# A graph network's second edge pass: rows prescaled by the attention vector, sums and absolute values on ScalarE

## The chip, the cores and the metric

The kernel runs on one core of a Trainium2 chip (trn2). The time is that of one execution on the device, in microseconds (us); the median of several runs counts.

## What is computed

Two graph layers over the same 103125 edges (50000 random ones in both directions and 3125 loops), 3125 nodes and 256 features; the edges come sorted by their destination.

```python
x = _layernorm(x + layer0(x, src, dst))      # attention with 8 heads over edges, then an MLP with GELU
x = _layernorm(x + layer1(x, src, dst))

def layer1(feature, src, dst, W_s, W_t, W_attn, W_fc, b_fc):
    proj_s = feature @ W_s.T
    proj_t = feature @ W_t.T
    z = proj_s[src] + proj_t[dst]
    z = where(z >= 0, z, 0.2 * z)
    e = (z @ W_attn.T)[:, 0]                 # one number an edge
    e_exp = exp(e - segment_max(e, src)[src])
    alpha = e_exp / segment_sum(e_exp, src)[src]
    msg = feature[src] * alpha[:, None]
    return segment_sum(msg, dst) @ W_fc.T + b_fc
```

The change lies in `e`, the edge score of layer 1, and in the tables of rows that it reads.

## The kernel before

One program, its engines coupled by semaphores that are written out by hand; nothing is scheduled by a tool. The stages, with their place in the profiled execution:

- 0 to 150 us: tables of the graph, and the q, k, v rows of layer 0, stored as rows in DRAM.
- 150 to 1535: **pass one**, the edges of layer 0.
- 1535 to 1890: **node stage**, five batches of 5 x 128 nodes: MLP, norms, and the two projections of layer 1. Per 128 nodes ScalarE copies both from PSUM (L1305, L1306) into `row` and `target`, VectorE multiplies both by 0.2 x attn and sums them (L1640, L1642) into one column more each; `split` (L1464 and the line behind) cuts `target` into three bfloat16 parts, and SyncE stores `row` and `x1` as `proj_rows` (514 float32 an edge's source), `row` alone as `narrow_rows` (258), and the parts as `part_rows`.
- 1890 to 3136: **pass two**, the edge scores of layer 1.
- 3136 to 3826: **pass three**, weighted sums of features by destination, output.

An edge tile is 128 edges, one per partition. A **visit** is 30 tiles, taken as 15 pairs p = 0 to 14; pass two has 27 visits. In a visit of pass two:

- GpSimd issues one indirect gather per tile (`gather_pair`, L793), 18 of wide rows of `proj_rows` and 12 of `narrow_rows`, into 15 pair slots (rooms `sb_ring`, `sb_w`, `sb_slots`). The gather for pair p of a visit may start when pair p of the visit before has been used (`slots_free`). It is thus up to a visit ahead.
- ScalarE makes the one-hot matrices that pick the destination node of each edge (`node_distances` L1178, `node_onehots` L1183; five of each, 768 columns), a visit ahead, and one Exp (L1324) for the visit before.
- TensorE expands the destination's part rows to edges with those one-hots (`expand`, L916): six matmuls a pair, three parts each, into PSUM `px`. It runs up to three pairs ahead of VectorE. At the last five pairs it also adds 6 matmuls each of the softmax denominators of the visit before (`denominators`, L1052).
- VectorE, per pair: `rows(p)` (L1699) adds gathered row and expanded row into `zbuf` (five pairs deep) and frees slot and PSUM; `attend(p)` copies the two extra columns (COPY, L1704) and makes one product with accumulator per tile (L1706): max(z, 0) x 0.8 attn. The leaky relu is 0.2 z + 0.8 max(z, 0), and the first term comes summed from the node stage in that extra column. Another extra column says if the edge's destination lies in the visit's window of nodes. Between the pairs stand `weighed` steps for the visit before, by the table `WEIGHED`: `low` (L1683, a comparison over 3840 columns), `high` (L1668), the split of the exponentials in three parts and `spread` (L1687, 2250 columns). Behind pair 14 come four operations on 30 columns (L1730, L1732, L1733, L1738).
- SyncE loads indices, destinations and part rows, and writes the source's features from `proj_kept` to `x_edges` for pass three.

Each engine works through its own queue in order; the order of the work around the change is the order in which these functions are written.

## Time and profile before

| | |
|---|---|
| runs | 3196.54, 3208.22, 3199.06 us |
| median | 3199.06 us |
| span of the profiled execution | 3825.7 us (19.6% over the median) |
| busy in it: TensorE, VectorE, ScalarE, GpSimd | 2265.8, 2190.3, 1162.1, 2033.0 us |
| DMA | 698.67 MB in 365776 packets |

The profiled execution has no time of its own beside its span. The span is read from the records of the engines; the runs were timed without a profile. In the rows below PE is TensorE (matmul), PEld its weight load, DVE VectorE, ACT ScalarE, POOL GpSimd, SP SyncE, and a "q" behind a name is the engine's sequencer. The bracket behind a row of a timeline, or what stands behind the second bar of a group, is the idle time ahead and what ended it. L793 is line 793 of the kernel before.

### The profile page before, as it was taken

The page shows a single profiled execution, that of the slowest core. Times are in us where ns is not written, and L with a number is a line of the kernel's source. Part 1 is how long each engine was busy: PE and PEld are TensorE (multiplying, and loading weights), DVE is VectorE, ACT ScalarE, POOL GpSimd, SP SyncE. Part 2 cuts the span into 40 slices and gives each one's busy share as a digit, 9 for nine tenths or more (in the row PEclk, how much of TensorE's full clock was granted, in tenths as well). Part 3 has the DMA queues.
Part 4 walks back from the last instruction along what each step waited for, and adds up shares of the span by engine and source line. Part 5 has one row for each costly group of instructions (what it writes and reads, how often), then busy time and mean ns, then how long its engine had stood idle before and what let it go on. Part 6 is the DMA issues. An engine that isn't in the chain of part 4 may idle for free.

```text
span 3825.7 us, 55082 instructions
## 1 busy us (share of the span) xinstructions
PE 2265.8 (59%) x11461; PEld 1680.5 (44%) x11462; DVE 2190.3 (57%) x6388; ACT 1162.1 (30%) x2751; POOL 2033.0 (53%) x1970
## 2 busy tenths in 40 slices
PE   4566666666666666587534445444444446777777
PEld 2244444444454444475423323332322235565565
DVE  5466556565665666234245556555555576666766
ACT  0145545554554555243212212222222210111111
POOL 0255555555565554212366676767776635444443
PEclk9788878887888788798766666666666668889988
DMA  4666666666666664122477777777777765666665
GB/s 139 208 174 183 177 184 185 179 185 181 185 183 188 187 181 129 54 69 74 139 205 217 219 218 216 213 212 216 212 213 215 211 209 187 194 193 199 202 199 171
DMA packets 365776, 698.67 MB, mean 183 GB/s; under 512 B 77382, under 2 KB 247104, under 8 KB 365739
## 3 DMA queue, kind: packets, MB, share of 16 engines
q0 software_dynamic: 134784, 425.63, 38.2%
q1 hardware_dynamic: 220666, 256.40, 21.4%
q10 hardware_dynamic: 10288, 16.23, 1.2%
q8 instruction: 12, 0.20, 0.0%
q14 instruction: 26, 0.21, 0.0%
HBM read 597.23 MB, written 100.85 MB: 182 GB/s over the span
## 4 chain that ended last, share of the span: by engine, by line
PE 31%; another core or an unknown queue 23%; DVE 21%; issue 16%; DMA 3%; DVEq 2%; SPq 2%; ACT 1%; POOL 1%; ACTq 0%; POOLq 0%
PE ps_px L916 10%; DVE sb_score L1517 4%; PE ps_pa L929 3%; PE ps_px L929 3%; DVE sb_prod L1706 3%; PE ps_pn L1052 3%; PE ps_px L1014 2%; DVE sb_wide L1699 2%; PE ps_px L1023 2%; PE ps_pa L1093 2%; DVE sb_wide L1526 1%; PE ps_px L892 1%; DVE sb_prod L1511 1%; DVE sb_parts L1911 1%
## 5 line engine op out<-in xcount | busy, mean ns | idle before, releaser
L916 PE MATMUL ps_px<-sb_parts 128*128 x2430 | 457.1, 349 | 609.8 <-DVE sb_wide L1699 465.4
L916 PEld LDWEIGHTS ps_px<-sb_parts 128*128 128x128 bf16 x2430 | 276.8, 121 | 757.2 <-DVE sb_wide L1699 490.7
L793 POOL DMA_INDIRECT sb_ring<-proj_rows,sb_idx x324 | 360.5, 1113 | 281.8 <-issue 164.1
L793 POOL DMA_INDIRECT sb_ring<-kv_rows,sb_idx x324 | 320.4, 989 | 338.4 <-DVE sb_wide L1526 131.5
L929 PE MATMUL ps_pa<-sb_wide,sb_onehot 128*128 128x264 f32 x864 | 300.5, 480 | 260.4 <-DVE sb_wide L1526 201.3
L793 POOL DMA_INDIRECT sb_parts<-kv_rows,sb_idx x324 | 316.0, 975 | 204.0 <-DVE sb_wide L1526 102.1
L916 PE MATMUL ps_px<-sb_parts,sb_xwm 128*128 x2430 | 399.9, 310 | 31.6 <-issue 14.8
L793 POOL DMA_INDIRECT sb_w<-narrow_rows,sb_idx x324 | 348.7, 1076 | 101.0 <-issue 97.5
L929 PE MATMUL ps_px<-sb_wide,sb_onehot 128*128 128x264 f32 x756 | 257.9, 474 | 201.6 <-DVE sb_wide L1526 141.0
L1699 DVE TENSOR_TENSOR sb_wide<-ps_px,sb_ring 128x516 f32<-128x516 f32 x162 | 109.6, 687 | 431.1 <-remote 392.2
L916 PEld LDWEIGHTS ps_px<-sb_parts,sb_xwm 128*128 128x128 bf16 x2430 | 271.4, 112 | 163.9 <-issue 63.3
L929 PEld LDWEIGHTS ps_pa<-sb_wide,sb_onehot 128*128 128x128 f32 x864 | 183.6, 234 | 315.7 <-DVE sb_wide L1526 189.1
L1197 ACT ACTIVATE sb_onehot<-sb_bits 128x256 f32<-128x256 bf16 x405 | 165.6, 409 | 489.8 <-remote 326.1
L793 POOL DMA_INDIRECT sb_w<-feat_rows,sb_idx x162 | 158.2, 977 | 293.5 <-PE ps_px L1093 132.0
L1706 DVE SCALAR_TENSOR_TENSOR sb_prod<-sb_wide,sb_attn_hi 128x256 f32<-128x256 f32 x810 | 309.1, 417 | 0.0
L1178 ACT ACTIVATE sb_parts<-sb_bits,sb_nn_tab 128x768 bf16<-128x768 int16 x135 | 126.0, 935 | 578.1 <-PE ps_px L916 397.7
L1190 ACT ACTIVATE sb_bits<-sb_iota_w,sb_ndst_f 128x128 bf16<-128x128 f32 x810 | 278.1, 389 | 39.7 <-issue 26.2
L1517 DVE TENSOR_REDUCE sb_score<-sb_prod 128x16 f32<-128x512 f32 x405 | 272.9, 674 | 0.0
L929 PEld LDWEIGHTS ps_px<-sb_wide,sb_onehot 128*128 128x128 f32 x756 | 160.4, 234 | 250.2 <-issue 117.4
L1911 DVE TENSOR_SCALAR sb_parts<-sb_iota_n,sb_dst_g,sb_ex_g 128x128 f32<-128x128 f32 x810 | 219.0, 355 | 35.6 <-issue 34.3
L1511 DVE TENSOR_TENSOR sb_prod<-ps_px,sb_ring 128x512 f32<-128x512 f32 x162 | 111.0, 685 | 221.0 <-remote 118.7
L1511 DVE TENSOR_TENSOR sb_prod<-ps_px,sb_parts 128x512 f32<-128x512 f32 x162 | 110.8, 684 | 208.5 <-remote 145.4
(265 smaller groups left out, 4535.1 us busy)
## 6 DMA issues: line engine op xcount, KB each, us to landing
sb_bits<-dst_short SPq DMA_DIRECT2D x280, 192.0 KB
x_edges<-sb_ring SPq DMA_DIRECT2D x54, 768.0 KB
sb_slots<-x_edges SPq DMA_DIRECT2D x54, 768.0 KB
x_edges<-sb_slots SPq DMA_DIRECT2D x27, 768.0 KB
sb_w<-x_edges SPq DMA_DIRECT2D x27, 768.0 KB
sb_msg<-lo_rows SPq DMA_DIRECT2D x28, 576.0 KB
kv_rows<-sb_slots ACTq DMA_DIRECT2D x25, 256.0 KB, 2.9
sb_parts<-part_rows SPq DMA_DIRECT2D x28, 193.5 KB
```

Source lines behind the costliest of these rows:

```text
L793: pool.indirect_dma_start(out=out[:, i, :], out_offset=None, in_=rows, in_offset=bass.IndirectOffsetOnAxis(ap=idx[:, 2 * p + i:2 * p + i + ...
L916: mm = pe.matmul(into, hots_t[L][:, 2 * p + i, :], flat(visit_parts[:, bass.ds(parity, 1), a, 0:width]), start=(a == 0), stop=(a == 2))
L929: mm = pe.matmul(into[:, 0:C + H], onehot[:, j, :], sums_in[:, 2 * (p % FLIGHT) + i, :], start=(p % EARLY == 0 and i == 0), stop=True, ski ...
L1052: mm = pe.matmul(pn[:, 0:3 * W], lo_hot[:, :, j], hi_ex[:, :, :, j].rearrange("p a n -> p (a n)"), start=False, stop=True, skip_group_chec ...
L1178: act.activation(hots_t[L][:, half(h), :], drow[:, h], ACT.Abs, bias=nn_tab[:, bass.ds(v, 1)]).then_inc(far[L], 1)
L1190: ins = act.activation(away[:, j, :], iota_w[:], ACT.Abs, bias=ndst_f[:, bass.ds(t0 + (2 * p + i), 1)])
L1197: act.activation(onehot[:, places(p), :], away[:, places(p), :], ACT.Relu, bias=1.0, scale=-1.0).then_inc(hot[0], 1)
L1511: dve.tensor_tensor(prod[:, p % 3].rearrange("p (j c) -> p j c", j=2), px[:, p % FLIGHT, :].rearrange("p (j c) -> p j c", j=2), kv_pairs[p ...
L1517: dve.tensor_reduce(score[:, p % FLIGHT], prod[:, p % 3].rearrange("p (j h d) -> p j h d", j=2, h=H), AX, ALU.add).then_inc(red1, 1)
L1699: dve.tensor_tensor(zbuf[:, pair(p), :], px[:, places(p), 0:CW], proj_slots(p)[:, :, 0:CW], ALU.add).then_inc(slots_free[1], 1)
L1706: ins = dve.scalar_tensor_tensor(out=prod[:, p % 3, i * C:i * C + C], in0=zbuf[:, 2 * (p % FLIGHT) + i, 0:C], scalar=0.0, in1=attn_hi[:], ...
L1911: ins = dve.tensor_scalar(weights[:, j, :], iota_n[:], dst_g[:, j:j + 1], ex_g[:, j:j + 1], ALU.is_equal, ALU.mult)
```

## The change

- In the node stage VectorE multiplies both projections by attn on their way out of PSUM; ScalarE's copies and the two products with accumulator are gone, and so are the two extra columns. Rows are 512 and 256 wide.
- Since z is now already z x attn, the leaky score is 0.6 x sum(z) + sum(|z| x 0.4 sign(attn)). ScalarE makes the first sum (Identity with accumulator into `lines`, two of 256 columns a pair; its other output goes to `unread`) and |z| (Abs, 512 columns, into `msg`); VectorE's two products now take |z| and `attn_sign`. New semaphores `lined` (ScalarE to VectorE) and `attended` (back).
- Whether the destination lies in the visit's window is now worked out on VectorE from the destination's number (`dst`, `above`, `inside`).
- PSUM holds five pairs ahead, one bank each, instead of three.
- The denominators are three matmuls a pair from p = 3 to 12, for the visit two back.
- The `weighed` steps move from p = 1 to 7 to p = 7 to 12. ScalarE's one-hots stand between its pairs.
- GpSimd gets a wait on the expansion (`expanded`) at p = 0, 5 and 10.

```diff
-CW = C + 2
-ROW = CW + C
+ROW = 2 * C
+EVEN = (1.0 + SLOPE) / 2.0
+ODD = (1.0 - SLOPE) / 2.0
...
-        attn_lo = sb("attn_lo", [P, C])
-        attn_hi = sb("attn_hi", [P, C])
+        attn_sign = sb("attn_sign", [P, C])
...
+        unread = onehot[:].rearrange("p j e -> p (j e)").bitcast(BF16).rearrange("p (j c) -> p j c", j=R)
         dots = sb("dots", [P, 3, G])
-        low_dots = sb("low_dots", [P, 2, G])
+        lines = sb("lines", [P, G])
...
-        NAS, NA = batch_steps(["hT*", "hid*", "sqrt1", "x1T*", "rows*"])
+        NAS, NA = batch_steps(["hT*", "hid*", "sqrt1", "x1T*"])
-        ZS = steps(["dots", "low", "masked", "kept", "added"])
+        ZS = steps(["dst", "above", "inside", "both", "masked", "kept", "added"])
...
+            def expanded(L, v, p):
+
+                pool.wait_ge(expd[L], v * PAIRS + p + PAIRS)
+                pool.sem_inc(pool_seen, 1)
...
                             pool.wait_ge(idx_in[1][p // SLOTS], v * 16 + 16)
+                            expanded(1, v, p)
...
-                    pe.wait_ge(slots_free[1], v * PAIRS + p + 1 + PAIRS - RING)
+                    pe.wait_ge(slots_free[1], v * PAIRS + p + 1 + PAIRS - FLIGHT)
-                    into = px[:, p % FLIGHT, i * C:i * C + width] if L == 0 else px[:, 2 * (p % RING) + i, 0:width]
+                    into = px[:, p % FLIGHT, i * C:(i + 1) * C]
...
-                for j in range(g * R, (g + 1) * R):
+                for j in range(g * THIRDS, (g + 1) * THIRDS):
...
-            def scored(v, earlier=None, second=False):
+            def scored(v, before=None, second=False):
-                    expand(1, CW, parity, v, p)
-                    if second and p == 2:
+                    expand(1, parity, v, p)
+                    if second and p == 7:
                         top_transposed()
-                    if second and p == 4:
+                    if second and p == 9:
                         top_spread()
-                    if earlier is not None and p >= PAIRS - HALVES:
-                        denominators(earlier, p - (PAIRS - HALVES))
+                    if before is not None and 3 <= p < 3 + S:
+                        denominators(before, p - 3)
...
-                scored(pe.snap(u + 2), pe.snap(u + 1))
-            for g in range(HALVES):
-                denominators(last_visit(pe), g)
+                scored(pe.snap(u + 2), u)
+            for v in (visit_before(pe), last_visit(pe)):
+                for g in range(S):
+                    denominators(v, g)
...
-                for s in range(NB):
-                    after_pe(it, "proj", s)
-
-                    act.wait_ge(proj_stored, it * (32 * NB) + 1)
-                    act.copy(row[:, s, 0:C], px[:, s % 4, 0:C])
-                    act.copy(target[:, s, 0:C], px[:, s % 4, C:2 * C]).then_inc(na, 1)
...
-            def node_half(v):
-                for h in range(HALVES):
-                    node_distances(1, v, h)
-                    if h:
-                        node_onehots(1, v, h - 1)
-                node_onehots(1, v, HALVES - 1)
+            def lined_up(v, p):
+
+                act.wait_ge(slots_free[1], v * PAIRS + p + 1 + PAIRS)
+                act.sem_inc(act_seen, 1)
+                act.wait_ge(attended, v * PAIRS + p + 1)
+                for i in (0, 1):
+                    act.activation(unread[:, 2 * (p % RING) + i], zbuf[:, 2 * (p % FLIGHT) + i, :], ACT.Identity, accum_out=lines[:, 2 * p + i:2 * p + i + 1])
+                act.activation(msg[:, places(p), 0:C], zbuf[:, pair(p), :], ACT.Abs).then_inc(lined, 1)
...
-            node_half(0)
-            with act.Fori(0, total - 1) as u:
-                node_half(act.snap(u + 1))
-                score_exps(u)
+            def scored(v, after=None, earlier=None):
+                for p in range(PAIRS):
+                    if p == 0 and earlier is not None:
+                        act.wait_ge(zs, earlier * len(ZS) + ZS["both"])
+                        act.sem_inc(act_seen, 1)
+                    lined_up(v, p)
+                    if earlier is not None and p == 6:
+                        score_exps(earlier)
+                    if after is not None and p % RING == 1 and p > 1:
+                        node_distances(1, after, p // RING - 1)
+                    if after is not None and p % RING == 2 and p > 2:
+                        node_onehots(1, after, p // RING - 1)
+                if after is not None:
+                    node_distances(1, after, HALVES - 1)
+                    node_onehots(1, after, HALVES - 1)
+
+            for h in range(HALVES):
+                node_distances(1, 0, h)
+                node_onehots(1, 0, h)
+            scored(0, 1)
+            with act.Fori(0, total - 2) as u:
+                scored(act.snap(u + 1), act.snap(u + 2), u)
+            scored(last_visit(act), earlier=visit_before(act))
...
-            dve.tensor_scalar(attn_lo[:], attn[:], SLOPE, None, ALU.mult).then_inc(tables, 1)
-            dve.tensor_scalar(attn_hi[:], attn[:], 1.0 - SLOPE, None, ALU.mult).then_inc(tables, 1)
+            dve.tensor_scalar(attn_sign[:], attn[:], 0.0, 2.0 * ODD, ALU.is_gt, ALU.mult).then_inc(tables, 1)
...
+            dve.tensor_scalar(attn_sign[:], attn_sign[:], -ODD, None, ALU.add).then_inc(tables, 1)
...
-                    dve.wait_ge(na, it * NA + NAS["rows", s])
-                    dve.scalar_tensor_tensor(out=prod[:, 0, 0:C], in0=px[:, s % 4, 0:C], scalar=1.0, in1=attn_lo[:], op0=ALU.mult, op1=ALU.mult,
-                                             accum_out=row[:, s, C:C + 1])
-                    dve.scalar_tensor_tensor(out=prod[:, 1, 0:C], in0=px[:, s % 4, C:2 * C], scalar=1.0, in1=attn_lo[:], op0=ALU.mult, op1=ALU.mult,
-                                             accum_out=target[:, s, C:C + 1]).then_inc(ndot, 1)
-                    dve.wait_ge(ndot, it * NB + s + 2)
-
-                split(target, CW, (W // NB + it) * SPLITS + 1, W // NB + it)
+                    dve.wait_ge(nt, it * NT + NTS["proj", s])
+                    dve.tensor_tensor(row[:, s], px[:, s % 4, 0:C], attn[:], ALU.mult)
+                    dve.tensor_tensor(target[:, s], px[:, s % 4, C:2 * C], attn[:], ALU.mult).then_inc(ndot, 1)
+
+                dve.wait_ge(ndot, it * NB + NB + 1)
+                split(target, C, (W // NB + it) * SPLITS + 1, W // NB + it)
...
-                    dve.wait_ge(dpe, v * HALVES + HALVES)
+                    dve.wait_ge(dpe, v + 1)
...
-            WEIGHED = {1: ["low"], 3: ["ex"], 4: ["part0"], 5: ["left1"], 6: ["part1", "high"], 7: ["left2", "part2", "spread"]}
+            WEIGHED = {7: ["ex"], 8: ["part0"], 9: ["left1", "low"], 10: ["part1", "high"], 11: ["left2"], 12: ["part2", "spread"]}
...
-                    dve.tensor_tensor(zbuf[:, pair(p), :], px[:, places(p), 0:CW], proj_slots(p)[:, :, 0:CW], ALU.add).then_inc(slots_free[1], 1)
+                    dve.tensor_tensor(zbuf[:, pair(p), :], px[:, p % FLIGHT, :].rearrange("p (j c) -> p j c", j=2),
+                                      proj_slots(p)[:, :, 0:C], ALU.add).then_inc(slots_free[1], 1)
                 def attend(p):
-                    dve.wait_ge(slots_free[1], v * PAIRS + p + 1 + PAIRS)
-                    dve.tensor_copy(low_dots[:, :, 2 * p:2 * p + 2].rearrange("p c j -> p j c"), zbuf[:, pair(p), C:CW])
+                    dve.wait_ge(lined, v * PAIRS + p + 1)
                     for i in (0, 1):
-                        ins = dve.scalar_tensor_tensor(out=prod[:, p % 3, i * C:i * C + C], in0=zbuf[:, 2 * (p % FLIGHT) + i, 0:C], scalar=0.0, in1=attn_hi[:],
-                                                       op0=ALU.max, op1=ALU.mult, accum_out=dots[:, 0, 2 * p + i:2 * p + i + 1])
-                    if p == PAIRS - 1:
-                        ins.then_inc(zs, 1)
+                        ins = dve.scalar_tensor_tensor(out=prod[:, p % 3, i * C:i * C + C], in0=msg[:, 2 * (p % RING) + i, 0:C], scalar=1.0, in1=attn_sign[:],
+                                                       op0=ALU.mult, op1=ALU.mult, accum_out=dots[:, 0, 2 * p + i:2 * p + i + 1])
+                    ins.then_inc(attended, 1)
...
                 rows(0)
+                rows(1)
                 for p in range(PAIRS):
-                    if p + 1 < PAIRS:
-                        rows(p + 1)
+                    if p + 2 < PAIRS:
+                        rows(p + 2)
                     attend(p)
-                    if second and p == 0:
+                    if p < 3:
+                        inside(("dst", "above", "inside")[p])
...
-                dve.wait_ge(zs, at("dots"))
-                dve.tensor_tensor(dots[:, 1], dots[:, 0], low_dots[:, 0], ALU.add).then_inc(zs, 1)
-                dve.wait_ge(zs, at("low"))
-                dve.tensor_tensor(dots[:, 2], dots[:, 1], low_dots[:, 1], ALU.mult).then_inc(zs, 1)
-                dve.tensor_copy(kept, low_dots[:, 1]).then_inc(zs, 1)
+                dve.wait_ge(attended, v * PAIRS + PAIRS + RING)
+                dve.scalar_tensor_tensor(out=dots[:, 0], in0=lines[:], scalar=EVEN, in1=dots[:, 0], op0=ALU.mult, op1=ALU.add).then_inc(zs, 1)
+                dve.wait_ge(zs, at("both"))
+                dve.tensor_tensor(dots[:, 2], dots[:, 0], dots[:, 1], ALU.mult).then_inc(zs, 1)
+                dve.tensor_copy(kept, dots[:, 1]).then_inc(zs, 1)
                 dve.wait_ge(zs, at("kept"))
```

Three places show how the instructions stand. **ScalarE**, in the loop of pass two. Before, at the start of a visit's turn: the distances (L1178) and one-hots (L1183) of the next visit follow each other.

```order
L1176 ISA [waits drow_in1_0]
L1178 ISA [waits expd1]
L1178 ACT_TABLE_LOAD
L1178 ACTIVATE sb_parts<-sb_bits,sb_nn_tab 128x768
L1176 REGISTER_ALU [waits drow_in1_1]
L1178 ACTIVATE sb_parts<-sb_bits,sb_nn_tab 128x768 [waits expd1]
L1182 ISA
L1183 ACTIVATE sb_parts<-sb_parts 128x768 [waits far1]
L1176 REGISTER_ALU [waits drow_in1_2]
L1178 ACTIVATE sb_parts<-sb_bits,sb_nn_tab 128x768 [waits expd1]
L1182 REGISTER_ALU
L1183 ACTIVATE sb_parts<-sb_parts 128x768 [waits far1]
```

After (L1324 is the sum, L1325 the absolute value, L1188 the distances, L1193 the one-hots):

```order
L1325 ACTIVATE sb_msg<-sb_wide 128x2x256
L1185 ISA
L1186 ISA [waits drow_in1_0]
L1188 ISA [waits expd1]
L1188 ACTIVATE sb_parts<-sb_bits,sb_nn_tab 128x768
L1320 REGISTER_ALU
L1322 REGISTER_ALU [waits slots_free1]
L1324 ACTIVATE sb_onehot,sb_lines<-sb_wide 128x256 [waits attended]
L1324 ACTIVATE sb_onehot,sb_lines<-sb_wide 128x256
L1325 ACTIVATE sb_msg<-sb_wide 128x2x256
L1192 ISA
L1193 ACTIVATE sb_parts<-sb_parts 128x768 [waits far1]
```

Each group of distances and one-hots now stands behind the sums of a pair and ahead of the next one's.

**VectorE**, pairs in the middle of a visit. Before (L1699 row add, L1704 copy of the extra columns, L1706 product):

```order
L1699 TENSOR_TENSOR sb_wide<-ps_px,sb_w 128x2x258 [waits gathered10,expd1]
L1704 COPY sb_low_dots<-sb_wide 128x2x2 [waits slots_free1]
L1706 SCALAR_TENSOR_TENSOR sb_prod,sb_dots<-sb_wide,sb_attn_hi 128x256 x2
L1699 TENSOR_TENSOR sb_wide<-ps_px,sb_w 128x2x258 [waits gathered11,expd1]
L1704 COPY sb_low_dots<-sb_wide 128x2x2 [waits slots_free1]
L1706 SCALAR_TENSOR_TENSOR sb_prod,sb_dots<-sb_wide,sb_attn_hi 128x256 x2
L1699 TENSOR_TENSOR sb_wide<-ps_px,sb_slots 128x2x258 [waits gathered12,expd1]
L1704 COPY sb_low_dots<-sb_wide 128x2x2 [waits slots_free1]
L1706 SCALAR_TENSOR_TENSOR sb_prod,sb_dots<-sb_wide,sb_attn_hi 128x256 x2
```

After (L1723 row add, L1730 product):

```order
L1723 TENSOR_TENSOR sb_wide<-ps_px,sb_w 128x2x256 [waits gathered9,expd1]
L1730 SCALAR_TENSOR_TENSOR sb_prod,sb_dots<-sb_msg,sb_attn_sign 128x256 [waits lined]
L1730 SCALAR_TENSOR_TENSOR sb_prod,sb_dots<-sb_msg,sb_attn_sign 128x256
L1723 TENSOR_TENSOR sb_wide<-ps_px,sb_w 128x2x256 [waits gathered10,expd1]
L1730 SCALAR_TENSOR_TENSOR sb_prod,sb_dots<-sb_msg,sb_attn_sign 128x256 [waits lined]
L1730 SCALAR_TENSOR_TENSOR sb_prod,sb_dots<-sb_msg,sb_attn_sign 128x256
L1723 TENSOR_TENSOR sb_wide<-ps_px,sb_w 128x2x256 [waits gathered11,expd1]
L1730 SCALAR_TENSOR_TENSOR sb_prod,sb_dots<-sb_msg,sb_attn_sign 128x256 [waits lined]
L1730 SCALAR_TENSOR_TENSOR sb_prod,sb_dots<-sb_msg,sb_attn_sign 128x256
```

The copy is gone, and the product waits for ScalarE in place of VectorE's own row add.

**TensorE**, denominators. Before, at the last pairs of a visit:

```order
L916 MATMUL ps_px<-sb_parts 128x258 [waits slots_free1]
L916 MATMUL ps_px<-sb_parts 128x258 x5
L1052 MATMUL ps_pn<-sb_parts 128x75 x6
L912 REGISTER_ALU
L916 MATMUL ps_px<-sb_parts 128x258 [waits slots_free1]
L916 MATMUL ps_px<-sb_parts 128x258 x5
L1052 MATMUL ps_pn<-sb_parts 128x75 x6
```

After, at p = 3 to 5 (L924 expansion, L1060 denominators):

```order
L924 MATMUL ps_px<-sb_parts 128x256 [waits slots_free1]
L924 MATMUL ps_px<-sb_parts 128x256 x5
L1058 REGISTER_ALU
L1060 MATMUL ps_pn<-sb_parts 128x75 [waits dv]
L1060 MATMUL ps_pn<-sb_parts 128x75 x2
L920 REGISTER_ALU
L924 MATMUL ps_px<-sb_parts 128x256 [waits slots_free1]
L924 MATMUL ps_px<-sb_parts 128x256 x5
L1060 MATMUL ps_pn<-sb_parts 128x75 x3
L920 REGISTER_ALU
L924 MATMUL ps_px<-sb_parts 128x256 [waits slots_free1]
L924 MATMUL ps_px<-sb_parts 128x256 x5
L1060 MATMUL ps_pn<-sb_parts 128x75 x3
```

Six behind each of five pairs became three behind each of ten, and the wait for VectorE's weights (`dv`) is now for a visit further back.

## Rows read from the trace of the kernel before

**Rows 1.** Windows of pass one, node stage, pass two, pass three; columns in the first line.
```profile
core 0: us, PE busy (x) PEld busy (x) DVE busy (x) ACT busy (x) POOL busy (x), PEclk, DMA share, GB/s
150.00:1535.00 1385.00, 894.47 (x4264) 653.01 (x4264) 814.66 (x1810) 695.18 (x1973) 795.35 (x810) 0.81 0.62 180
1535.00:1890.00 355.00, 266.93 (x1449) 210.70 (x1450) 121.59 (x343) 123.19 (x359) 74.35 (x35) 0.87 0.23 75
1890.00:3136.00 1246.00, 533.78 (x3168) 373.07 (x3166) 697.32 (x2753) 255.37 (x310) 846.47 (x795) 0.66 0.72 212
3136.00:3826.00 690.00, 490.53 (x2368) 400.50 (x2368) 472.04 (x1332) 88.33 (x109) 315.53 (x325) 0.87 0.60 195
```
**Rows 2.** Timeline of GpSimd (POOL) over a visit's end and start, pass two.
```profile
2458.09 0.95 POOL L793 DMA_INDIRECT sb_slots<-proj_rows,sb_idx  x1 [0.30 <-issue]
2463.57 1.01 POOL L793 DMA_INDIRECT sb_ring<-proj_rows,sb_idx  x1 [4.53 <-DVE sb_wide L1699]
...
2466.25 2.12 POOL L793 DMA_INDIRECT sb_ring<-proj_rows,sb_idx  x1 [0.30 <-issue]
```
**Rows 3.** Timeline of VectorE (DVE) at the same place.
```profile
2445.13 0.19 DVE L1738 TENSOR_TENSOR sb_e_all<-sb_e_all,sb_dots 128x30 f32 x1
2462.06 1.30 DVE L1699 TENSOR_TENSOR sb_wide<-ps_px,sb_ring 128x516 f32<-128x516 f32 x2 [16.74 <-remote]
...
2464.03 0.69 DVE L1699 TENSOR_TENSOR sb_wide<-ps_px,sb_ring 128x516 f32<-128x516 f32 x1
2464.64 0.16 DVE L1704 COPY sb_low_dots<-sb_wide 128x4 f32<-128x4 f32 x1
2464.70 0.42 DVE L1706 SCALAR_TENSOR_TENSOR sb_prod<-sb_wide,sb_attn_hi 128x256 f32<-128x256 f32 x1
```
**Rows 4.** One line of SyncE, 2443 to 2461 us: min/median/max ns; then between 2400 and 2442.
```profile
L582 SPq ALU_OP  x2: 697/699/701, 2445.7 to 2458.4; - x2
...
L582 SPq ALU_OP  x4: 13/364/700, 2400.0 to 2419.8; - x4
```
**Rows 5.** Costliest groups in pass two: line, engine, shapes, count | busy, mean | idle before.
```profile
L793 POOL DMA_INDIRECT sb_ring<-proj_rows,sb_idx x315 | 351.0, 1114 | 214.2 <-DVE sb_wide L1699 101.9 <-issue 96.4 <-DMA sb_idx<-in_src 15.8
L793 POOL DMA_INDIRECT sb_w<-narrow_rows,sb_idx x318 | 341.6, 1074 | 99.1 <-issue 95.7 <-DVE sb_wide L1699 3.5
L1706 DVE SCALAR_TENSOR_TENSOR sb_prod<-sb_wide,sb_attn_hi 128x256 f32<-128x256 f32 x802 | 306.0, 417 | 0.0
...
L793 POOL DMA_INDIRECT sb_slots<-proj_rows,sb_idx x162 | 153.9, 950 | 52.5 <-issue 49.2 <-DVE sb_wide L1699 3.3
...
L1704 DVE COPY sb_low_dots<-sb_wide 128x4 f32<-128x4 f32 x401 | 84.0, 209 | 0.0
L1706 DVE DVE_READ_ACCUMULATOR sb_prod<-sb_wide,sb_attn_hi 128x1 f32 x802 | 63.3, 79 | 0.0
```
**Rows 6.** Groups of ScalarE (ACT) in the whole run, shapes kept apart.
```profile
L1197 ACT ACTIVATE sb_onehot<-sb_bits 128x256 f32<-128x256 bf16 x405 | 165.6, 409 | 489.8 <-remote 326.1 <-PE ps_pa L929 69.8 <-PE ps_px L929 45.0
L1178 ACT ACTIVATE sb_parts<-sb_bits,sb_nn_tab 128x768 bf16<-128x768 int16 x135 | 126.0, 935 | 578.1 <-PE ps_px L916 397.7 <-remote 142.9 <-issue 37.2
...
L1183 ACT ACTIVATE sb_parts<-sb_parts 128x768 bf16<-128x768 bf16 x135 | 109.1, 827 | 0.0
...
L1178 ACT ACT_TABLE_LOAD x26 | 33.4, 1283 | 356.5 <-remote 343.6 <-PE ps_px L916 12.2 <-issue 0.7
...
L1336 ACT COPY sb_tr<-ps_pn 128x256 f32<-128x256 f32 x27 | 10.1, 373 | 443.0 <-PE ps_pn L1111 236.8 <-remote 206.2
...
L1338 ACT ACTIVATE sb_rstd<-sb_mv,sb_eps 128x1 f32<-128x1 f32 x27 | 7.9, 294 | 144.9 <-DVE sb_mv L1889 76.1 <-DVE sb_hn L1884 34.0 <-issue 17.6
```
**Rows 7.** Groups of the denominators and of the row add of pairs in slots, pass two.
```profile
L1052 PE MATMUL ps_pn<-sb_parts 128*128 128x75 bf16 x780 | 127.3, 311 | 98.7 <-DVE sb_parts L1687 91.3 <-issue 7.4
...
L1699 DVE TENSOR_TENSOR sb_wide<-ps_px,sb_slots 128x516 f32<-128x516 f32 x81 | 56.4, 696 | 99.6 <-PE ps_px L916 56.7 <-remote 34.9 <-issue 7.8
```
**Rows 8.** Timeline of VectorE at the end of the node stage.
```profile
1863.97 0.42 DVE L1640 SCALAR_TENSOR_TENSOR sb_prod<-ps_px,sb_attn_lo 128x256 f32<-128x256 f32 x1 [0.94 <-ACT sb_wide L1306]
```

92 lines of the change are left out of this document (53 added, 39 removed).

## The prediction

> **What bounds the kernel now.** I read the stages first, one row of windows each [rows 1]. Pass two, which the change rewrites, is 1246 us of the span. No engine is full there: GpSimd is busy 846 us, VectorE 697, TensorE 534, ScalarE 255. The busy shares don't name the bound, so I went to GpSimd's timeline over one visit [rows 2]. Its 30 gathers follow one another without a gap other than 0.30 us of issuing, and then it stands 4.53 us until VectorE has added the first pair of the next visit. VectorE's timeline of the same moment [rows 3] shows the reverse: it ended its visit at 2445.3, stood 16.74 us, and began when the last gather had gone out, 3.97 us after 2458.09. A visit so takes 45.8 us: the gathers, then a handover.
>
> That handover is, I think, the recorder's and not the kernel's. The profiled execution lasted 3825.7 us, 626.6 more than the median of 3199.06, and in those gaps SyncE's simplest register instruction takes 697 to 701 ns, and 13 ns at other times [rows 4]; nothing in the program can hold such an instruction. Without it VectorE follows the gathers closely, and GpSimd never stands. Its own work per visit is then 30 x (846.47 / 795 + 0.305) = 41.1 us, 27 visits 1110 us. As a test, pass one by the same rule: 795.35 + 810 x 0.305 = 1042. With 150 us ahead of it and 355 for the node stage that makes 2657 and leaves 542 of the median's 3199 for pass three, whose TensorE is busy 490.5 [rows 1]. That closes, so the model for a timed run is: **pass two goes at the pace of GpSimd's gathers, 41.1 us a visit.** The sum below is made as a difference on this, since the span of the profiled execution holds 626 us that timed runs don't have; I set it on the median.
>
> **The change part by part.** *VectorE in pass two.* Gone are 15 COPYs a visit (209 ns each by the groups [rows 5]). In the timeline the product (at 2464.70) starts 0.06 us after the COPY (2464.64) [rows 3], so on VectorE's own chain a COPY costs 0.06 to 0.21 us, a visit 0.9 to 3.1. Added are three operations on 30 columns (dst, above, inside), like the row of 0.19 us at 2445.13 [rows 3], 0.6 together; the two products per pair (417 ns [rows 5]) stay, with other operands, and the row add loses 4 of 516 columns. VectorE's load, 697.32 / 27 = 25.8 us a visit, falls to 23 to 25. Below 41.1 this is hidden: 0.
>
> *ScalarE in pass two.* Today a visit is 5 x 0.935 + 5 x 0.827 + 1.283, and an Exp over 30 columns that I price like the one-column instruction, 0.294: 10.4 us [rows 6]. Added per pair are two Identity passes over 256 columns with an accumulator and one Abs over 512. Nothing in the trace has an accumulator on ScalarE. An operation of 256 columns took 373 (COPY) to 409 ns (L1197), one of 768 took 827, so one of 512 about 0.618 by the line between 409 and 827. For reading an accumulator I take VectorE's 79 ns [rows 5] as the low end and ScalarE's own one-column instruction, 294 ns [rows 6], as the high one. A pair is 2 x 0.373 + 0.618 + 2 x 0.079 = 1.52 to 2 x 0.409 + 0.618 + 2 x 0.294 = 2.02. I take 1.85, nearer the high end, since a one-column instruction of the same engine is the closer relative. The visit: 15 x 1.85 + 10.4 = 38.1 us, with ends 33.2 and 40.7. All three lie under 41.1, so ScalarE is hidden: 0, but with 3 us in hand. It goes from the idlest engine to the second busiest; if GpSimd's cover went away, this would be the next bound.
>
> *TensorE.* Expansion loses 2 of 258 columns; the denominators are the same 30 matmuls a visit, three a pair from p = 3, for the visit two back. Today they wait for the spread: 91.3 us in the whole pass [rows 7]. They wait no more, but TensorE's 534 / 27 = 19.8 us a visit isn't the pace either: 0. Running five pairs ahead instead of three takes away waits of VectorE for TensorE, 56.7 us at the pairs in slots [rows 7]; under GpSimd's pace also 0. Behind the loop stand 60 matmuls in place of 30: 30 x 127.3 / 780 = 4.9 us more, whose first half is ready while VectorE still makes the last weights. Between 0 and 4.9 I take +1.
>
> *GpSimd.* Each gathered row is 8 bytes shorter (2056 to 2048, 1032 to 1024), 0.4 to 0.8% of the bytes; the engine's 0.95 us is the same for both widths [rows 2, 5], so the size isn't what it takes: 0. It gets a wait for TensorE at p = 0, 5 and 10: all pairs ahead of p must be expanded. For p = 0 that is the whole visit before, and with five pairs of PSUM it asks for that visit's row add 9; for p = 10 it asks for row add 4 of the same visit, gathered from 6 pairs ago, over 13.7 us (5 x 41.1 / 15). VectorE starts 3.97 us after a gather's start at the latest [rows 2, 3], so there is room: 0, with its own rival below. SyncE's queue gets one wait behind pass two for the low rows; they are needed later: 0.
>
> *Ends.* The last pair of the pass now goes from row add through ScalarE (1.85) to the products, and the products of the pair before (0.8) lie beside it: +1. *Node stage:* ScalarE's two copies per 128 rows and VectorE's two products with accumulator become two plain products from PSUM. The five batches go at TensorE's pace but for the last, where VectorE stands 0.94 us for ScalarE's copy ahead of each pair of products [rows 8]: -0.9 once.
>
> The sum: 3199 + 0 (27 visits) + 1 + 1 - 0.9 = 3200 us. The measurement of this kernel can tell about 0.5% (16 us) from no change, so this is "same".
>
> **The rivals.**
> *A, ScalarE becomes the bound (slower).* Place: the chain row add, three ScalarE operations, products. Price: the high end of 40.7, plus 0.15 us a pair if the waits cost ScalarE's sequencer half of GpSimd's issue time (0.30 [rows 2]), 2.2: 42.9 a visit, + 1.8 x 27 = +49, so 3248. It decides from a pair of about 2.05 us on. For it: nothing shows the accumulator's price, and the one-hots stand in the same queue in front of pairs. Against: five buffers take up jitter. The Trainium skill speaks against the change too ("ScalarE: Activation LUTs", rules for kernel authors): relu, max, min, add and mul belong on VectorE, not ScalarE. It gives a speed per element and no price of an accumulator, so by itself it doesn't say which engine ends last here.
> *B, GpSimd gets faster.* A gather beside running VectorE work takes longer: 1.01 us against 0.95, and 2.12 beside the comparison over 3840 columns [rows 2]. If the COPYs do part of this, I bound it by the excess of the means over 950 ns: 164 and 124 ns [rows 5], of which up to 100 ns for each of 15 pairs: 1.5 x 27 = 40 us, 3159. For it: gathers into ring and w have means of 1114 and 1074 ns, into slots, where VectorE mostly rests, 950 [rows 5]. Against: the long operations, which stay, explain much of it. The Trainium skill ("SBUF — State Buffer", who interferes with whom) says that a copy in a two-port mode and an operation with two SBUF inputs hold off GpSimd's access, and by it this rival holds for the COPYs while the products, with two SBUF inputs before and after, stay as they were. The same shift of VectorE's operations against the gathers can go either way by 0.7 us a visit, 19 us.
> *C, the visits hang on VectorE's and TensorE's chain in timed runs.* Then the COPYs (15 x 0.06 = 0.9 less 0.6 for the added operations, by the starts, and 3.1 less 0.6 by the durations: 0.3 to 2.5 us a visit, middle 1.4, 38 us in all) and the five-ahead expansion (56.7 us [rows 7]) count: 3199 - 95 = 3104. Against: VectorE's load is 25.8 of 41.1.
> *D, the new GpSimd wait binds.* If a timed visit also began VectorE's work only when the last gather had gone out, as the profiled one did, GpSimd would stand until row add 9: a visit's work on VectorE is 45.8 - 16.7 = 29 us, nine pairs of it 17.5, times 27 is 470, so 3670. It decides once VectorE is over 9 pairs behind. I give it little, as it needs the recorder's stalls in timed runs.
>
> **How the numbers follow.** Forecast 0.44, A 0.18, B 0.19, C 0.13, D 0.06. Faster by over 0.5%: B + C = 0.32; within 0.5%: 0.44; slower: A + D = 0.24. The forecast alone spans 3180 to 3220 (the 19 us of the shift). The range takes in A (3248) and B (3159), each with that shift,, and leaves out C and D, 0.19 together: 3140 to 3270.
>
> **What the profile of the changed kernel would show.** Right: GpSimd's gathers still back to back at 1.25 us with a mean near 1.0 to 1.1; ScalarE busy near 38 us a visit, so near 1000 us in pass two; VectorE's products rarely waiting for `lined`. The accumulator's row gives A's disputed price. B: gathers into ring and w with a mean clearly under 1.1 us. D, or its likeness from the recorder alone: GpSimd standing at the visit's start and at p = 5 or 10 on TensorE's expansion; the profiled span could grow by hundreds of us while timed runs do not. Wrong: timed runs beyond 3140 or 3270, or gathers that wait on ScalarE's chain.

## The result and the profile after

| | before | after |
|---|---|---|
| runs | 20 | 20 |
| median | 3202.36 us (3196.54 to 3216.70) | 3208.77 us (3202.77 to 3216.39) |
| ratio, 95% interval | | 1.0023 (1.0014 to 1.0031) |
| span of the profiled execution | 3825.7 us | 3209.2 us |

The kernel is 6.4 us slower, 0.23%, within the 0.5% that I called no change; 3200 was forecast. The profiled execution of the changed kernel took 3211.07 us, like its other runs. That of the kernel before did not: its 3825.7 us are what the kernel before takes on some chips, in timed runs too. In the runs below its median was 3202 us on one chip and 3833, 3884 and 3895 us on three others; two executions of it, 6030.32 and 8994.58 us, lie far outside the rest and are left out of the ratios. So the rows of before and those of after come from different conditions, and I needed the kernel before once more from a chip like the one of the timed runs (`before_third`, 3199.27 us) to compare them. Here are its windows by stage, then those of the changed kernel (columns as in [rows 1]).

```profile
153.00:1217.00 1064.00, 782.68 (x4222) 560.54 (x4222) 819.52 (x1785) 697.20 (x1952) 816.69 (x810) 0.96 0.78 233
1217.00:1575.00 358.00, 268.61 (x1444) 211.14 (x1442) 121.19 (x340) 124.89 (x373) 57.99 (x21) 0.88 0.19 63
1575.00:2668.00 1093.00, 624.40 (x3215) 391.05 (x3215) 718.69 (x2758) 260.93 (x316) 846.16 (x810) 0.60 0.84 244
2668.00:3197.00 529.00, 436.81 (x2368) 363.47 (x2368) 469.32 (x1355) 88.64 (x110) 323.21 (x325) 0.95 0.78 260
```

```profile
152.00:1225.00 1073.00, 779.87 (x4216) 561.60 (x4216) 820.45 (x1783) 697.07 (x1949) 826.42 (x810) 0.96 0.78 231
1225.00:1581.00 356.00, 272.92 (x1450) 214.18 (x1448) 118.45 (x285) 115.26 (x329) 58.03 (x21) 0.87 0.19 63
1581.00:2677.00 1096.00, 618.20 (x3185) 396.35 (x3185) 690.52 (x2426) 797.06 (x2321) 849.03 (x810) 0.61 0.80 242
2677.00:3209.00 532.00, 445.43 (x2398) 368.45 (x2398) 473.32 (x1365) 92.94 (x125) 320.38 (x326) 0.94 0.78 259
```

Pass one is the same code in both and differs by 9 us, so single executions differ by as much in a stage. GpSimd's busy time in it, the last engine column, differs by as much too (816.69 and 826.42), and its gathers follow one another without a gap over 0.4 us there as well. The node stage gives 2 us, pass two costs 3, the rest 3. Pass two is 27 visits at 1093 / 27 = 40.5 us before and 1096 / 27 = 40.6 after; the forecast had 41.1 for both. GpSimd's groups in pass two, before and after, which answer to [rows 5]:

```profile
L793 POOL DMA_INDIRECT sb_w<-narrow_rows,sb_idx x324 | 367.9, 1136 | 98.7 <-issue 92.3 <-DVE sb_wide L1699 6.4
L793 POOL DMA_INDIRECT sb_ring<-proj_rows,sb_idx x324 | 319.0, 985 | 163.7 <-issue 160.6 <-DVE sb_wide L1699 3.0
...
L793 POOL DMA_INDIRECT sb_slots<-proj_rows,sb_idx x162 | 159.5, 984 | 49.4 <-issue 45.1 <-DVE sb_wide L1699 4.3
```

```profile
L795 POOL DMA_INDIRECT sb_ring<-proj_rows,sb_idx x324 | 342.0, 1056 | 161.3 <-issue 156.7 <-DVE sb_wide L1723 3.4 <-PE ps_px L924 1.2
...
L795 POOL DMA_INDIRECT sb_w<-narrow_rows,sb_idx x324 | 315.4, 973 | 98.8 <-issue 89.3 <-DVE sb_wide L1723 8.2 <-PE ps_px L924 1.2
...
L795 POOL DMA_INDIRECT sb_slots<-proj_rows,sb_idx x162 | 191.8, 1184 | 49.4 <-issue 46.0 <-DVE sb_wide L1723 3.0 <-PE ps_px L924 0.3
```

Idle time ahead of them is nearly all `issue`: 0.305 us a gather, 810 x 0.305 = 247. With 849.2 us busy that makes 1096, the whole stage. GpSimd never stands in these two executions: no gap over 0.4 us in 810 gathers. The work that moved is seen on ScalarE and VectorE of the changed kernel:

```profile
L1324 ACT ACTIVATE sb_onehot<-sb_wide 128x256 bf16<-128x256 f32 x804 | 325.0, 405 | 238.9 <-DVE sb_wide L1723 237.6
...
L1730 DVE SCALAR_TENSOR_TENSOR sb_prod<-sb_msg,sb_attn_sign 128x256 f32<-128x256 f32 x801 | 304.3, 419 | 1.4 <-ACT sb_msg L1325 1.4
...
L1325 ACT ACTIVATE sb_msg<-sb_wide 128x512 f32<-128x512 f32 x402 | 246.9, 614 | 0.0
...
L1324 ACT ACTIVATION_READ_ACCUMULATOR sb_onehot<-sb_wide 128x1 f32 x804 | 150.1, 187 | 0.0
```

ScalarE is busy 797 us in place of 261 (L1324 is the sum, its READ_ACCUMULATOR row the part that writes the sum out, L1325 the absolute value), and VectorE's products (L1730) waited 1.4 us for it in the whole pass.

Where the gathers' time above the bare 0.947 us goes can be read from timelines. Two places of the changed kernel, GpSimd and then VectorE:

```profile
2225.33 1.07 POOL L795 DMA_INDIRECT sb_slots<-proj_rows,sb_idx  x1 [0.30 <-DVE sb_wide L1723]
2226.70 2.22 POOL L795 DMA_INDIRECT sb_slots<-proj_rows,sb_idx  x1 [0.30 <-issue]
2229.22 0.98 POOL L795 DMA_INDIRECT sb_slots<-proj_rows,sb_idx  x1 [0.30 <-issue]
...
2233.24 0.94 POOL L795 DMA_INDIRECT sb_ring<-proj_rows,sb_idx  x1 [0.30 <-issue]
2234.49 1.98 POOL L795 DMA_INDIRECT sb_ring<-proj_rows,sb_idx  x1 [0.30 <-issue]
2236.77 1.06 POOL L795 DMA_INDIRECT sb_ring<-proj_rows,sb_idx  x1 [0.30 <-issue]
```

```profile
2225.95 2.15 DVE L1707 TENSOR_TENSOR sb_parts<-sb_parts,sb_src_lob 128x3840 bf16<-128x3840 bf16 x1
2228.02 0.68 DVE L1723 TENSOR_TENSOR sb_wide<-ps_px,sb_slots 128x512 f32<-128x512 f32 x1
...
2234.32 1.33 DVE L1711 TENSOR_TENSOR sb_parts<-sb_parts 128x2250 bf16<-128x2250 bf16 x1
2235.56 0.42 DVE L1730 SCALAR_TENSOR_TENSOR sb_prod<-sb_msg,sb_attn_sign 128x256 f32<-128x256 f32 x1
```

The comparison L1707 runs from 2225.95 to 2228.10; the gather that starts in it at 2226.70 takes 2.22 us. The spread L1711 starts at 2234.32; the gather at 2234.49 takes 1.98. In the kernel before (`before_third`) gathers fall into the spread as well, but later in it:

```profile
1889.74 1.39 POOL L793 DMA_INDIRECT sb_w<-narrow_rows,sb_idx  x1 [0.30 <-issue]
```

```profile
1888.98 1.33 DVE L1687 TENSOR_TENSOR sb_parts<-sb_parts 128x2250 bf16<-128x2250 bf16 x1
```

The same was done for all 810 gathers of pass two: each one's duration less 0.947 us (the usual gather in both traces) is put down to the VectorE operation that runs as it starts, and where two overlap there, to the one that began later. The table has the kernels of two experiments beside them, which are told below.

```
us in pass two              before_third   after   sign_psum   both_again
product, 256 columns            28.3        21.4       0.2        -0.4
comparison, 3840 columns        34.4        35.5      30.1         7.6 (pieces)
spread, 2250 columns            11.6        23.3      16.3         1.5 (pieces)
COPY of 4 columns                2.7          -         -           -
row add (one operand in PSUM)   -0.3         0.1       0.2        -0.3
no VectorE operation running     1.2         1.4       1.9         0.9
all gathers                     79.4        82.1      49.1         9.6
```

The rest of a column is small operations; a negative sum is only many gathers a nanosecond or two under 0.947. The column sign_psum is from a B-chip. How long a gather is held can be read too. In `after` 158 gathers were lengthened by over 0.1 us beside a running operation, and each by what was left of that operation as it started, less 0.125 us (0.122 to 0.130 for nine in ten of them); in before_third 206, less 0.128. So a gather that meets such an operation goes on when the operation ends. The COPY's 2.7 us are one gather, which started 0.02 us ahead of a product and was held through two products and the comparison behind them; the other ten beside a COPY weren't held.

### The profile page after: what moved, and what is told of

It reads as the page before. It is cut to its first block, busy times and chain, and to the rows that moved or that the text cites. A ratio compares the mean times of both kernels' runs of the same rounds, so it can differ in the third digit from the quotient of the medians.

```text
span 3209.2 us, 58358 instructions
## 1 busy us (share of the span) xinstructions
PE 2198.0 (68%) x11461; PEld 1584.7 (49%) x11462; DVE 2187.4 (68%) x6006; ACT 1703.2 (53%) x4725; POOL 2055.2 (64%) x1970
## 4 chain that ended last, share of the span: by engine, by line
POOL 30%; issue 21%; DMA 19%; PE 14%; DVE 13%; DVEq 1%; SPq 1%; POOLq 1%; ACT 1%; ACTq 0%
POOL sb_ring L795 12%; POOL sb_parts L795 7%; POOL sb_slots L795 5%; POOL sb_w L795 5%; DMA sb_slots<-kv_rows,sb_idx 4%; DMA sb_ring<-proj_rows,sb_idx 3%; DMA sb_w<-narrow_rows,sb_idx 3%; DMA sb_ring<-kv_rows,sb_idx 3%; PE ps_px L1022 3%; DVE sb_parts L1948 3%; PE ps_px L1031 3%; PE ps_px L1103 2%; PE ps_px L900 2%; DMA sb_msg<-lo_rows 2%; PE ps_pa L1103 1%
## 5 line engine op out<-in xcount | busy, mean ns | idle before, releaser
L924 PE MATMUL ps_px<-sb_parts 128*128 x2430 | 535.6, 388 | 378.3 <-DVE sb_wide L1723 376.3
L924 PEld LDWEIGHTS ps_px<-sb_parts 128*128 128x128 bf16 x2430 | 292.3, 130 | 567.1 <-DVE sb_wide L1723 346.0
L1324 ACT ACTIVATE sb_onehot<-sb_wide 128x256 bf16<-128x256 f32 x810 | 327.4, 405 | 242.4 <-DVE sb_wide L1723 241.1
L937 PE MATMUL ps_pa<-sb_wide,sb_onehot 128*128 128x264 f32 x864 | 256.1, 420 | 150.9 <-DVE sb_wide L1551 136.9
L924 PE MATMUL ps_px<-sb_parts,sb_xwm 128*128 x2430 | 346.4, 281 | 17.6 <-ACT sb_xwm L1193 14.6
L937 PE MATMUL ps_px<-sb_wide,sb_onehot 128*128 128x264 f32 x756 | 221.0, 418 | 139.4 <-DVE sb_wide L1551 138.5
L1730 DVE SCALAR_TENSOR_TENSOR sb_prod<-sb_msg,sb_attn_sign 128x256 f32<-128x256 f32 x810 | 307.6, 419 | 1.4 <-ACT sb_msg L1325 1.4
L924 PEld LDWEIGHTS ps_px<-sb_parts,sb_xwm 128*128 128x128 bf16 x2430 | 244.6, 101 | 108.5 <-issue 20.8
L1723 DVE TENSOR_TENSOR sb_wide<-ps_px,sb_w 128x512 f32<-128x512 f32 x162 | 111.5, 688 | 210.6 <-DMA sb_w<-narrow_rows,sb_idx 209.8
L1325 ACT ACTIVATE sb_msg<-sb_wide 128x512 f32<-128x512 f32 x405 | 248.8, 614 | 0.0
L1060 PE MATMUL ps_pn<-sb_parts 128*128 128x75 bf16 x810 | 152.8, 311 | 105.9 <-DVE sb_parts L1711 105.9
L795 POOL DMA_INDIRECT sb_slots<-proj_rows,sb_idx x162 | 191.8, 1184 | 49.4 <-issue 46.0
```

The lines of the kernel that those rows point to most:

```text
L795: pool.indirect_dma_start(out=out[:, i, :], out_offset=None, in_=rows, in_offset=bass.IndirectOffsetOnAxis(ap=idx[:, 2 * p + i:2 * p + i + ...
L924: mm = pe.matmul(into, hots_t[L][:, 2 * p + i, :], flat(visit_parts[:, bass.ds(parity, 1), a, :]), start=(a == 0), stop=(a == 2))
L937: mm = pe.matmul(into[:, 0:C + H], onehot[:, j, :], sums_in[:, 2 * (p % FLIGHT) + i, :], start=(p % EARLY == 0 and i == 0), stop=True, ski ...
L1060: mm = pe.matmul(pn[:, 0:3 * W], lo_hot[:, :, j], hi_ex[:, :, :, j].rearrange("p a n -> p (a n)"), start=False, stop=True, skip_group_chec ...
L1324: act.activation(unread[:, 2 * (p % RING) + i], zbuf[:, 2 * (p % FLIGHT) + i, :], ACT.Identity, accum_out=lines[:, 2 * p + i:2 * p + i + 1])
L1325: act.activation(msg[:, places(p), 0:C], zbuf[:, pair(p), :], ACT.Abs).then_inc(lined, 1)
```

## The experiments

Twelve runs of nine kernels were made, in four sets; each set has its own runs of the kernel before on its chip. A-chip stands for one where that takes about 3200 us, B-chip for one where it takes over 3800.

**before_again** (first set, B-chip) is the kernel before, unchanged.

> The kernel before once more, for a second profiled execution. Theory (the 16.7 us gaps of VectorE came from the recorder): if this execution is not held up, its span is near 3200 us, GpSimd's gathers stand back to back for all of pass two at about 41 us a visit, and VectorE starts a visit 1 to 2 pairs behind the gathers, not at the last one. Rival (the gaps are the kernel's own handover): visits of about 45.8 us and VectorE starting with the last gather again, whatever the span.

Measured: 3828.88 us, span 3827.0, and the kernel before timed at 3833.15 (median of 29). Visits of 45.7 us, VectorE starting each 3.9 us after the start of the last gather, as in the first profile (4.0; medians of 24 visits). The theory of the recorder can't be kept as I put it: timed runs on this chip take just as long, so it isn't a thing of one profiled execution. `before_third` shows that the rival isn't right for A-chips either.

**before_third** (third set, A-chip) is the same kernel.

> The kernel before a third time, to see what one of its executions of about 3200 us looks like, if the chip gives one. Theory (GpSimd's gathers set the pace and a gather costs 0.947 us, 0.30 of issue and what VectorE's operations with two SBUF inputs add): pass two has 27 visits of 40 to 41.5 us with no gap between gathers, as the changed kernel had at 40.6. Rival C (the visits hang on VectorE's and TensorE's chain): gathers with gaps, in pass two over 30 us of them. If the execution takes about 3830 us again, it says nothing new.

Measured: 3199.27 us. Visits of 40.5 us, no gap between gathers, VectorE's first row add of a visit starts 5.1 us after GpSimd has issued the visit's first pair, and 31.8 us ahead of the last gather. This is the model of the prediction, and rival C is out. One line of SyncE's queue tells the two kinds of chip apart: this kernel here, and the changed one on a B-chip (durations in ns, least, median, most).

```profile
L582 SPq ALU_OP  x108: 32/36/45, 1588.3 to 2657.2; - x108
```

```profile
L584 SPq ALU_OP  x108: 14/41/728, 1913.0 to 3154.6; - x108
```

The first never takes over 45 ns, the second now and then 728. The windows of the changed kernel on the B-chip:

```profile
152.00:1532.00 1380.00, 869.44 (x4163) 641.74 (x4164) 792.11 (x1753) 680.44 (x1924) 799.13 (x810) 0.80 0.62 179
1532.00:1900.00 368.00, 281.25 (x1503) 220.27 (x1501) 130.94 (x315) 122.89 (x354) 57.84 (x21) 0.88 0.19 61
1900.00:3155.00 1255.00, 586.52 (x3185) 392.95 (x3185) 680.34 (x2422) 812.18 (x2321) 832.98 (x810) 0.63 0.70 212
3155.00:3883.00 728.00, 506.52 (x2398) 413.22 (x2398) 482.84 (x1367) 92.90 (x125) 315.97 (x325) 0.84 0.59 190
```

Against the A-chip pass one takes 1380 us in place of 1073, pass two 1255 in place of 1096, pass three and the output 728 in place of 532; the node stage, whose DMA share is 0.19 against 0.6 to 0.8, 368 and 356. What makes the stages with much DMA traffic longer, and whether SyncE's slow instructions are its cause or its sign, stays open; no run here tells a property of the chip from one of how it is recorded.

**no_expanded** (first set, B-chip) takes GpSimd's new wait away.

```diff
-                            expanded(1, v, p)
```

> The changed kernel without GpSimd's new wait for TensorE at p = 0, 5 and 10. Theory (gathers set the pace, VectorE is at most 3 to 4 pairs behind them, so the wait is met when it comes; in the changed profile GpSimd stood 2.7 us for TensorE in all of pass two): 3203 to 3209 us, no difference beyond 0.2%. Rival D (the wait costs): it gets faster by what the wait costs, at least 6 us, so that it meets the kernel before or beats it.

**after_again** (second set, B-chip) is the changed kernel.

> The changed kernel itself, on the chip of these runs, where the kernel before takes 3833 us in place of 3202. Theory (the change costs and gives nothing under GpSimd's pace): ratio to the kernel before 1.000 to 1.005 here too. Rival D (GpSimd's new wait holds it wherever VectorE begins a visit with the last gather, as the profiled kernel before did on this chip): up to 17 us a visit, so 3900 to 4300 us, and the version without the wait, at 3846.5, is much faster than this one.

Measured: without the wait 1.0027 of the kernel before (1.0009 to 1.0046), with it 0.9981 (0.9964 to 0.9998). The two ran on different chips, each against the kernel before on its own, so they don't measure the wait's price to 0.5%; but the hundreds of us of rival D are excluded. Its premise was right for B-chips, and the traces show it. Without the wait VectorE began a visit 42.4 us after its first pair had been issued, that is with the last gather, as the kernel before does there; with it 7.6 us after. GpSimd's groups in pass two, without the wait and with it:

```profile
L795 POOL DMA_INDIRECT sb_w<-narrow_rows,sb_idx x324 | 342.8, 1058 | 154.6 <-issue 92.5 <-DVE sb_wide L1722 61.5 <-remote 0.6
```

```profile
L795 POOL DMA_INDIRECT sb_w<-narrow_rows,sb_idx x324 | 316.9, 978 | 201.9 <-DVE sb_wide L1723 96.8 <-issue 86.2 <-PE ps_px L924 14.9
```

GpSimd stands in both: gaps of over 0.4 us between gathers sum to 193 us without the wait, at many places of a visit, and to 192 with it, 182 of them at p = 0 and 10, where the wait is. So the wait binds on a B-chip, but takes from GpSimd what it would stand anyway: gathers are not the pace there. On the A-chip GpSimd stood 2.7 us for TensorE in all. The changed kernel without the wait was not run on an A-chip.

**sign_psum** (first set, B-chip) puts the vector of the products into the PSUM bank that the change left free.

```diff
-  ... scalar=1.0, in1=attn_sign[:],
+  ... scalar=1.0, in1=px[:, 5, 0:C],
...
+            dve.tensor_copy(px[:, 5, 0:C], attn_sign[:]).then_inc(signs_in, 1)
+            dve.wait_ge(signs_in, 1)
             scored(0)
```

> The changed kernel with the sign vector in PSUM (a bank that pass two leaves free), so that VectorE's 810 products have one operand in SBUF and one in PSUM. Theory (a gather that GpSimd starts while VectorE runs an operation with two SBUF inputs is held until that ends, and gathers set the pace): the changed profile has 14 to 20 us of lengthened gathers beside these products in pass two; they go, so 3208.8 falls to 3189 to 3195 (ratio to the kernel before 0.996 to 0.998). Rival (gathers are lengthened by any VectorE work, or by DMA traffic): no change, 3206 to 3211.

Measured: 0.9954 (0.9937 to 0.9971), a little faster than the 0.996 to 0.998 expected, on a chip where gathers aren't the pace. This ratio is no proof: in the profiled executions pass two took 1235.5 us from its first gather to its last, against 1233.1 in before_again, and the 18 us by which the span is shorter lie behind pass two, whose code the edit leaves alone (703 and 726 us). The mechanism is shown by the trace: 223 gathers started beside a product and were lengthened by 0.001 us on the mean, 0.2 us in all, against 241 by 0.089 us in the changed kernel. The products take as long as before (415 ns, and 419). So it is the second SBUF operand that holds the gather, not VectorE's being busy; the row adds, with one operand in PSUM in every kernel, say the same (198 gathers beside them in `after`, 0.1 us in all). The Trainium skill states this ("SBUF — State Buffer", who interferes with whom): a VectorE operation with two SBUF inputs contends with a GpSimd instruction that reads SBUF; the trace agrees, 0.089 against 0.001 us a gather.

**pieces** (first set, B-chip) cuts the two long operations.

```diff
-  dve.tensor_tensor(lo_hot, low_iota, src_lob[...]..., ALU.is_equal)
+  dve.tensor_tensor(lo_hot[:, some], low_iota[:, some], ..., ALU.is_equal)     # some: a quarter
...
-  WEIGHED = {7: ["ex"], 8: ["part0"], 9: ["left1", "low"], 10: ["part1", "high"], 11: ["left2"], 12: ["part2", "spread"]}
+  WEIGHED = {7: ["ex"], 8: ["part0", "low0"], 9: ["left1", "low1"], 10: ["part1", "low2"], 11: ["left2", "high", "low3"],
+             12: ["part2", "spread0"], 13: ["spread1", "spread2"]}
```

> The changed kernel with VectorE's comparison over 3840 columns cut into four pieces of 960 and the spread over 2250 columns into three of 750, one or two behind a pair. Same work, and about 5 fixed costs of 0.1 us more a visit on VectorE. Theory (a gather waits for the end of the VectorE operation that it starts in; in the changed profile these two operations lengthened gathers by about 50 us in 27 visits): with pieces of 0.45 to 0.6 us about 20 us are left, so 3208.8 falls by some 28 us to 3175 to 3186 (ratio to the kernel before 0.991 to 0.995). Rival (VectorE, ScalarE or DMA sets the pace): no change or up to 10 us slower.

Measured: 0.9986 (0.9964 to 1.0007), no gain that the interval shows, where 0.991 to 0.995 was expected. Gathers were lengthened by 34.6 us in all (57.5 in no_expanded on the same chip), but GpSimd stood the longer: gaps between gathers of over 0.4 us sum to 214 us in its pass two, against 193.

**both** (second set, B-chip) and **both_again** (third set, A-chip) have the two edits together.

> The changed kernel with the sign vector in PSUM and the two long VectorE operations in pieces. Theory (both take away lengthened gathers, each its own): the gains add up, 0.995 x 0.9986 over the changed kernel's own ratio: 0.990 to 0.994 of the kernel before, and gathers of pass two lengthened by under 25 us in all, against 82 in the changed profile. Rival (only one of them counts, since a gather missed by one is caught by the other): no better than 0.9954.

> The sign vector in PSUM and the pieces once more, beside a kernel before that, if the chip gives it, takes about 3200 us. Theory (under the gathers' pace, lengthened gathers are paid in full): 82 us of lengthening fall to under 30 as in the profile of the first run, so 3209 falls by about 50 us: 3155 to 3170, ratio 0.985 to 0.990. Where the kernel before takes over 3800 us, engines are held up for other reasons and the gain is hidden: ratio 0.995 to 1.002, as the first time. Rival (lengthened gathers are no cost even under the gathers' pace): ratio 1.000 to 1.003 with the kernel before at 3200 us.

Measured: on the B-chip 0.9999 (0.9978 to 1.0021), where 0.990 to 0.994 was expected; on the A-chip **3128.88 us, 0.9774 (0.9760 to 0.9788)**, five runs. It beats both kernels, by 73 us the one before. The profile of the run on the A-chip, by stage, and GpSimd's groups in its pass two:

```profile
1570.00:2593.00 1023.00, 594.86 (x3185) 386.63 (x3185) 694.25 (x2553) 792.89 (x2322) 776.32 (x810) 0.65 0.85 260
```

```profile
L796 POOL DMA_INDIRECT sb_ring<-proj_rows,sb_idx x324 | 310.6, 959 | 161.2 <-issue 156.9 <-DVE sb_wide L1728 3.7 <-PE ps_px L925 0.6
L796 POOL DMA_INDIRECT sb_w<-narrow_rows,sb_idx x324 | 307.6, 949 | 98.7 <-issue 86.8 <-DVE sb_wide L1728 11.0 <-PE ps_px L925 0.9
...
L796 POOL DMA_INDIRECT sb_slots<-proj_rows,sb_idx x162 | 158.4, 978 | 49.3 <-issue 47.8 <-DVE sb_wide L1728 1.5
```

Pass two is 1023 us in place of 1096; the lengthening fell from 82.1 to 9.6, which is these 73 us. So lengthened gathers are paid in full where gathers set the pace. I expected 50 us, since I had left 30 of lengthening; 11 more came in pass one, whose code is the same (1062 against 1073): its gathers were lengthened by 48.2 us in all, and by 59.8 in `after`. On the B-chip another limit stands behind the gathers: their lengthening fell from 66.1 us in after_again to 12.3, and the time that GpSimd stood in pass two (gaps over 0.4 us, less 0.305 each) rose from 175.4 to 231.3, so that the sum stayed, 241.5 and 243.6.

**act_plus1** and **act_plus4** (second set, B-chip), **act_plus4_again** (fourth set, B-chip) load ScalarE.

```diff
+  for k in range(4):        # act_plus1: one Abs over 512 columns
+      act.activation(more[:, p % RING, k * P:(k + 1) * P], zbuf[...128 columns of the pair...], ACT.Abs)
```

> The changed kernel with one more Abs over 512 columns per pair on ScalarE, into a scratch buffer, in front of the real one: 0.52 us a pair, 7.8 a visit, so ScalarE's chain goes from 29.7 us a visit (by the starts in the changed profile) to 37.5. Theory (ScalarE is hidden under GpSimd's 40.6 us): no change within 0.3% of the changed kernel. Rival A (ScalarE's chain is already at the pace): 7.8 x 27 = up to 210 us slower.

> The changed kernel with four more Abs over 128 columns per pair on ScalarE, into a scratch buffer: 0.29 us each by the starts, 17.4 us a visit, so ScalarE's chain is 47 us a visit. Theory: this crosses GpSimd's pace, ScalarE sets it, and pass two gets longer by 6.5 us a visit or more where gathers set the pace at 40.6, 175 us; where visits take 45.8 us, 1.3 a visit or more, 35 to 175 us. If it costs nothing, ScalarE's chain has more room than I read.

> The changed kernel with four more Abs over 128 columns per pair on ScalarE once more. Theory: ScalarE's chain of 29.7 us a visit gets 17.4 more, 47, against GpSimd's 40.6: + 6.4 x 26 = 165 us or more, ratio 1.05 to 1.08, and the gathers now stand for VectorE, which waits for ScalarE. Where the kernel before takes over 3800 us, + 80 us as the first time. Rival (ScalarE's chain is not what ended last, VectorE's products merely lag): under 1.03 with the kernel before at 3200 us.

Measured: 1.0009 (0.9991 to 1.0026), 1.0221 (1.0182 to 1.0260) and 1.0228 (1.0192 to 1.0265), where the changed kernel has 0.9981. One more operation is nearly free (0.3%; ScalarE is then busy 37.4 us a visit), four cost 2.4%, by the ratios of one chip. Groups and window of act_plus4's pass two:

```profile
1905.00:3241.00 1336.00, 623.35 (x3179) 392.55 (x3179) 692.33 (x2405) 1117.76 (x3891) 820.11 (x810) 0.59 0.67 199
```

```profile
L1327 ACT ACTIVATE sb_more<-sb_wide 128x128 bf16<-128x128 f32 x1591 | 363.8, 294 | 69.7 <-issue 68.2 <-DVE sb_wide L1726 1.1
...
L796 POOL DMA_INDIRECT sb_w<-narrow_rows,sb_idx x324 | 321.8, 993 | 280.8 <-PE ps_px L925 111.2 <-remote 87.1 <-issue 82.0
...
L1733 DVE SCALAR_TENSOR_TENSOR sb_prod<-sb_msg,sb_attn_sign 128x256 f32<-128x256 f32 x794 | 306.3, 423 | 592.1 <-remote 233.5 <-ACT sb_msg L1328 205.5 <-issue 153.0
```

The visit takes 1336 / 27 = 49.5 us where the changed kernel took 46.5 there; 47 was the chain by the starts. VectorE's products now stand 205.5 us for ScalarE, and GpSimd stands 111.2 us for TensorE: the wait of rival D and the bound of rival A show when ScalarE is loaded. None of the three met an A-chip, so the 1.05 expected there wasn't tried, nor was one more operation against a visit of 40.6 us. act_plus4_again met what its expectation says for a B-chip (+ 80 us; it was + 89).

**before_both** (fourth set, B-chip) gives the old kernel the same cures.

```diff
-  WEIGHED = {1: ["low"], 3: ["ex"], 4: ["part0"], 5: ["left1"], 6: ["part1", "high"], 7: ["left2", "part2", "spread"]}
+  WEIGHED = {1: ["low0"], 2: ["low1"], 3: ["ex", "low2"], 4: ["part0", "low3"], 5: ["left1"], 6: ["part1", "high"],
+             7: ["left2", "part2", "spread0"], 8: ["spread1", "spread2"]}
...
-  ... scalar=0.0, in1=attn_hi[:],
+  ... scalar=0.0, in1=(attn_hi[:] if earlier is None or second else pa[:, C:2 * C]),
```

> The kernel before, without the change, with the two cures: its vector for the products in PSUM (beside TensorE's scratch, from the third visit on, since the other banks are full) and the two long VectorE operations in pieces. Theory (in both kernels GpSimd's gathers set the pace and VectorE's two-SBUF-input operations lengthen them; ScalarE's sums give nothing): 79 us of lengthening in its pass two fall to under 20, so 3202 falls to 3130 to 3150, ratio 0.977 to 0.984, close to the 0.977 that the changed kernel reached with the same cures. Rival (it is the change that makes the cures work): ratio above 0.990. Where the kernel before takes over 3800 us, only the lengthening in the trace can be read.

Measured: 1.0048 (1.0028 to 1.0068) on a B-chip. Lengthening fell to 20.5 us there, from 101.6 in before_again on another B-chip. So the cures take the lengthening away in the old kernel too, and on a B-chip that gives no time there either (0.5% slower by the ratio); what they are worth to it on an A-chip was not measured. If it is what it is in the changed kernel, the change itself is worth nothing: that is argued, not shown.

## Why the prediction was right

- *What bounds the kernel*: right. The gathers at 30 x (busy + 0.305) a visit, 41.1 us forecast, 40.5 and 40.6 measured, without gaps. The check of this model on the median was a weak one, though: pass three got what was left over, and the terms were off both ways. In before_third pass one took 1064 us and not 1042, pass two 1093 and not 1110, pass three 529 and not 542. That the sum closed was in part luck.
- *The reason for the profile's gaps* was wrong in part. I said that they were the recorder's and that timed runs have none. The runs that I was given have none, but timed runs on three other chips are as long as that profile, and their profiled executions have them. The forecast was safe from this because it was set on the median, not on the span.
- *VectorE*: hidden, as said. Its load fell from 26.6 to 25.6 us a visit (718.69 and 690.52 over 27), by less than the forecast's 23 to 25 from 25.8. The COPY's price to the gathers, rival B, is 2.7 us in before_third, not 40, and that is one gather beside a product; the prediction's reason for it, that the COPYs hold gathers off, isn't seen (28 gathers beside them in before_again, 0.001 us on the mean). The COPYs went and the products' share fell from 28.3 to 21.4, but the moved spread meets gathers earlier in it: 11.6 us before, 23.3 after. That is the "shift" of up to 19 us either way; net it is 79.4 against 82.1, + 3.
- *ScalarE*: the term of 1.85 us a pair was too high for what it was used for. Durations add up to 2 x 0.405 + 2 x 0.187 + 0.614 = 1.80, and the accumulator's 187 ns lie between my ends of 79 and 294. But operations overlap. ScalarE's timeline from one pair's first sum to the distances behind its Abs:

```profile
2224.05 0.42 ACT L1324 ACTIVATE sb_onehot<-sb_wide 128x256 bf16<-128x256 f32 x1 [3.51 <-DVE sb_wide L1723]
2224.38 0.19 ACT L1324 ACTIVATION_READ_ACCUMULATOR sb_onehot<-sb_wide 128x1 f32 x1
2224.47 0.40 ACT L1324 ACTIVATE sb_onehot<-sb_wide 128x256 bf16<-128x256 f32 x1
...
2224.87 0.61 ACT L1325 ACTIVATE sb_msg<-sb_wide 128x512 f32<-128x512 f32 x1
2225.39 0.92 ACT L1188 ACTIVATE sb_parts<-sb_bits,sb_nn_tab 128x768 bf16<-128x768 int16 x1
```

  By the starts a pair takes 1.34 us (2224.05 to 2225.39), a visit with its one-hots 29.7 and not 38.1. The profile's busy time says the same, 797.06 / 27 = 29.5, where the prediction looked for 38. So 11 us were in hand, not 3, and rival A deserved less than its 0.18. act_plus1 and act_plus4 put ScalarE's edge between 37 and 47 us on a chip where a visit takes 46.5; on an A-chip it is only known that 29.5 is hidden.
- *TensorE, the wait on the expansion*: 0 was right, one reason wasn't. "They wait no more" is false: TensorE still waits for the spread (84.2 us of idle time ahead of the denominators against 92.1); it costs nothing. That it waits because it now runs five pairs ahead is argued, not shown.
- *Ends and node stage*: -0.9 + 1 + 1. From the last gather of pass two to the first of pass three it takes 42 us after and 40 before; the node stage 356 and 358. The signs are right; the sizes are at the noise of one execution.
- *The measured + 6.4 us* can't be placed to the us. The two profiled executions differ by 11.8 us, and 9 of them are pass one, whose gathers were lengthened by 49.6 us in before_third and 59.8 in `after`; since both_again, with the changed kernel's pass one, has 48.2, this isn't the code of that pass. How gathers fall against VectorE's operations shifts each pass by some us, and the forecast counted it for pass two alone. That the sum came within 9 us of 3209 owes something to luck: + 1 + 1 - 0.9 is below what any such shift moves.

## What to carry to other kernels

When one engine issues back to back, its pace is its busy time plus its issue time, and a busy share of 77% is then full. Work that is moved off another engine gives nothing there; look instead at what lengthens the pacing instruction, operation by operation, by what runs as it starts. And before a gap in a profile is explained, ask if the profiled execution took the time of the runs.

## What the runs showed that I had not expected

- The same program takes 3200 us on some chips and 3830 to 3895 us on others, with nearly all of the difference (662 of 674 us between after_again and `after`) in the stages with much DMA traffic. What sets the pace there stays open; it isn't the gathers.
- A second operand in PSUM in place of SBUF takes a VectorE operation out of GpSimd's way entirely (0.089 to 0.001 us a gather) and costs the operation nothing (419 and 415 ns).
- A gather that starts beside a VectorE operation with two SBUF inputs is held until 0.13 us before that operation's end and then takes its usual 0.947 us; 364 gathers of two kernels fit this.
- Cutting a comparison of 3840 columns (2153 ns) in four costs VectorE 4 x 652 ns, 21% more, and frees 1.0 us of gathers a visit (35.5 to 7.6 us in 27 visits); together with the spread's pieces and the PSUM operand it was worth 2.5% of the kernel.
- ScalarE's operations with accumulator follow one another every 0.42 us though operation and accumulator read last 0.59 together.
